# A fused transformer block on one core: the attention's second product moves to the end of a slot of the layers, and its output projection behind the next tile's projection of q

## What is computed

```python
for i in range(6):
    t = shift_tokens(x)                       # half the channels come from the token before
    q, k, v = split(t @ Wqkv[i])              # 128 -> 3 * 1024
    q, k = rotary(l2norm(q) * qs), rotary(l2norm(k) * ks)
    x = local_attention(q, k, v) @ Wo[i] + x  # softmax over 64 keys, 1024 -> 128
    n = layernorm(shift_tokens(x)) * g + b
    a, gate = split(n @ W1[i] + b1)           # 128 -> 2 * 341
    x = (a * gelu(gate)) @ W2[i] + b2 + x
x = x_mid + gb * x
```

## Time and profile before

| | us |
|---|---|
| median of 3 runs | 3675.78 |
| lowest and highest | 3674.07 to 3676.65 |
| profiled execution, its own time | 3676.79 |
| span of its profile | 3675.0 |
| busy in the span: PE | 3518.1 (96%) |
| DVE | 3185.6 (87%) |
| ACT | 2870.5 (78%) |
| POOL | 2576.6 (70%) |

### The profile page before, as it was taken

The page is one execution under the profiler, slowest core; times in us unless marked ns, Lnnn a source line. Parts: engine busy times, 40 slices in busy tenths (PEclk is TensorE's granted clock), DMA queues, the critical chain, the costliest instruction groups (busy, mean ns, idle before and its releaser), DMA issues.

```text
span 3675.0 us, 161687 instructions
## 1 busy us (share of the span) xinstructions
PE 3518.1 (96%) x70540; PEld 2666.8 (73%) x70540; DVE 3185.6 (87%) x4422; ACT 2870.5 (78%) x5288; POOL 2576.6 (70%) x2106
## 2 busy tenths in 40 slices
PE   6999999869999999999999999999999999999996
PEld 2222222358888888888888888888888888888885
DVE  7999999578888988888888889888888888888884
ACT  3999999857777787877777787878777777777774
POOL 3222111278888888888888888888888888888883
PEclk8999999989999999999999999999999999999999
DMA  4110000034444444444444444444444444444432
GB/s 121 40 42 22 23 20 19 16 96 111 122 115 110 126 116 117 117 113 114 128 115 120 113 115 127 113 118 114 114 122 120 117 118 111 132 119 111 115 111 73
DMA packets 210250, 366.48 MB, mean 100 GB/s; under 512 B 37106, under 2 KB 81734, under 8 KB 209222
## 3 DMA queue, kind: packets, MB, share of 16 engines
q1 hardware_dynamic: 209482, 355.05, 35.1%
HBM read 236.73 MB, written 111.67 MB: 95 GB/s over the span
## 4 chain that ended last, share of the span: by engine, by line
PE 46%; DVE 14%; ACT 9%; issue 5%; POOL 5%; ACTq 0%; POOLq 0%; DVEq 0%
PE PB L1447 8%; PE PA L1371 8%; PE PD L1399 6%; PE PD L1460 5%; PE PB L1371 4%; PE PC L1421 4%; PE PC L1499 3%; DVE T L1756 3%; PE PA L1430 3%; PE PC L1475 2%; POOL T L1283 2%; DVE T L1746 2%; DVE T L1750 2%; DVE ss L1762 2%; ACT Vs L1565 1%
## 5 line engine op out<-in xcount | busy, mean ns | idle before, releaser
L1265 POOL TENSOR_TENSOR T<-T 128x1024 f32<-128x1024 f32 x384 | 907.3, 2379 | 8.7 <-DVE T L1756 8.7
L1283 POOL TENSOR_TENSOR T<-T,rn 128x1024 f32<-128x1024 f32 x384 | 731.4, 1905 | 27.7 <-POOL rn L1276 1.3
L1371 PE MATMUL PA<-Wqkv,XS 128*128 128x512 f32 x2304 | 633.0, 410 | 9.8 <-DVE XS L1710 9.1
L759 DVE TENSOR_REDUCE negmax<-p_max 128x1 f32<-128x1024 f32 x512 | 588.9, 1214 | 15.5 <-PE p_max L659 13.4
L821 ACT ACTIVATE E<-p_low 128x512 f32<-128x512 f32 x1024 | 554.0, 596 | 27.7 <-PE p_low L683 16.9
L1371 PEld LDWEIGHTS PA<-Wqkv,XS 128*128 128x128 f32 x2304 | 417.0, 194 | 80.7 <-DVE XS L1710 10.7
L1728 DVE TENSOR_REDUCE sm<-Ew 128x16 f32<-128x1024 f32 x192 | 233.6, 1217 | 236.7 <-ACT Ew L1589 236.7
L1762 DVE TENSOR_REDUCE ss<-SQ 128x32 f32<-128x2048 f32 x192 | 436.9, 2276 | 0.0
L1399 PE MATMUL PD<-ident,T 128*128 128x128 f32 x3072 | 410.7, 277 | 17.5 <-POOL T L1283 16.2
L1447 PEld LDWEIGHTS PB<-ET,VW 64*64 64x64 f32 x24576 | 376.4, 135 | 45.6 <-DVE T L1756 29.6
L1447 PE MATMUL PB<-ET,VW 64*64 64x32 f32 x24576 | 398.2, 220 | 10.6 <-DVE T L1756 5.2
(11 more groups left out here) (167 smaller groups left out, 6988.7 us busy)
## 6 DMA issues: line engine op xcount, KB each, us to landing
VW<-v_rows SPq DMA_DIRECT2D x768, 256.0 KB, 4.6
v_rows<-Vs SPq DMA_DIRECT2D x192, 512.0 KB, 3.4
Wraw<-in_Wqkv SPq DMA_DIRECT2D x40, 192.0 KB, 5.0
QA<-parts_q SPq DMA_DIRECT2D x384, 16.0 KB
KA<-parts_k SPq DMA_DIRECT2D x192, 32.0 KB
fs<-XC SPq DMA_DIRECT2D x48, 127.0 KB
parts_q<-AO SPq DMA_DIRECT2D x8, 384.0 KB, 2.6
parts_k<-AO SPq DMA_DIRECT2D x8, 384.0 KB, 3.3
```

The costliest lines, as they stand in the source:

```text
L759: dve.tensor_reduce(negmax[:, qh, c, qt:qt + 1], p_max[:, k % 2, :], axis=AX.X, op=ALU.max, negate=True).then_inc(s_mr.sem, 1)
L1265: pool.tensor_tensor(out=t_, in0=t_, in1=T2[:, i * HALF:(i + 1) * HALF], op=ALU.add).then_inc(ad.sem, 1)
L1283: pool.tensor_tensor(out=t_, in0=t_, in1=rn[:, p, i * LH:(i + 1) * LH].unsqueeze(2).broadcast_to([P, LH, LD]), op=ALU.mult).then_inc(no.se ...
L1371: mm = pe.matmul(pair[:, half, :], XS[:, b, i, 1:P + 1], Wqkv[:, l % 2, j, lo:lo + 512], start=(k == 0), stop=(k == 2))
```

## The change

On PE `attend(s-3)` goes from behind the transposition of k to the slot's end, behind `project_v` and the feed-forward's products of the slot. `output(s-4)` goes from ahead of `project_qk(s, 0)` to behind it, and the alignment goes with it. On ACT `project_v` and `exponentials` now come ahead of `attend`, and `roots` behind it. On DVE `output` stands behind the first half of `rotate`. SP waits for the output of tile `s-4` rather than for scores ahead of its transfers, and for the first copy of qT rather than the third copy (kT) ahead of reading the windows. No computation is added or removed.

```diff
@@ on_sp
-            if is_tile(s - 2):
-                sp.wait_ge(sc.sem, sc.at(s - 2))
+            if is_tile(s - 4):
+                sp.wait_ge(wo.sem, wo.at(s - 4))
             if is_tile(s - 1):
                 values_out(s - 1)
-                sp.wait_ge(te.sem, te.at(s - 1, 3))
+                sp.wait_ge(te.sem, te.at(s - 1, 1))
@@ layers
-    BLOCK, FIRST_Q = 256, (105, 105, 98, 98)
+    BLOCK, FIRST_OUT = 256, (51, 41, 39, 19)
@@ on_pe, project_qk
             if i == 0:
-                pe.addr_align(BLOCK, offset=FIRST_Q[b], max_nops=0)
                 pe.wait_ge(xl.sem, xl.at(n))
@@ on_pe, output
             u, b, t, l = tile(n)
+            pe.addr_align(BLOCK, offset=FIRST_OUT[b], max_nops=0)
             free(fd[0])
@@ on_pe, the loop
+            if is_tile(s):
+                project_qk(s, 0)
             if is_tile(s - 4):
                 output(s - 4)
-            if is_tile(s):
-                project_qk(s, 0)
...
                 transpose_qk(s - 1, 1)
-            if is_tile(s - 3):
-                attend(s - 3)
             if is_tile(s + 1):
                 input_T(s + 1)
...
                 ff_down(u - 2)
+            if is_tile(s - 3):
+                attend(s - 3)
@@ on_act, the loop
+            if is_tile(s):
+                project_v(s)
+            if is_tile(s - 2):
+                exponentials(s - 2)
             if is_tile(s - 3):
                 attend(s - 3)
             if is_tile(s):
-                project_v(s)
                 roots(s)
             if d == 0 and is_step(u - 2):
                 ff_norm(u - 2)
-            if is_tile(s - 2):
-                exponentials(s - 2)
@@ on_dve, the loop
+            if is_tile(s):
+                rotate(s, 0)
             if is_tile(s - 4):
                 output(s - 4)
...
             if is_tile(s):
-                rotate(s, 0)
                 rotate(s, 1)
```

More of the change, by code:

```diff
@@ L1696, in on_act @@
                 ff_norm(u - 2)
-            if is_tile(s - 2):
-                exponentials(s - 2)
-            if d == 0 and is_step(u - 2):
                 ff_high(u - 2)
```

## The result

| | before | after |
|---|---|---|
| median, us | 3675.59 | 4087.86 |
| lowest and highest | 3674.07 to 3676.65 | 4083.45 to 4095.98 |
| span of the profile | 3675.0 | 4094.2 |

The changed kernel takes 1.1125 times as long, interval [1.1105, 1.1144], that is 412 us more. The forecast was 301 more. The direction and the largest term were right, the sum was 111 us short, and the time lies above the range.

What follows compares the result with a forecast made beforehand. PE was taken to set the pace, busy 2469.7 of 2500 us in the layers. Terms 265 + 31 + 10 + 10 - 15 = 301 us on 3676.8 gave 3978, median forecast 3977 us; range for 8 in 10: 3880 to 4055 us.

Steps and rivals of the forecast that it cites:

- The wait for kH: On PE, `input_T` waits for ACT's kH copy out of PD once `attend` moves: 1.40 us, 189 slots, 265 us.
- Scores with d = 3: PE's scores wait for DVE's last `ff_value` product, now behind the rotation of q: 0.64 us in 48 steps, 31 us.
- The branch and SP's transfers: PE's one branch a slot stays at 0.29 us and SP's earlier window reads cost nothing: 0 us.
- whether OT is ready: `output` behind the projection of q: ACT's OT copy is covered by some 0.4 us, so no cost by itself.
- Roots behind the copy: ACT's roots wait for `attend`'s copy, delaying POOL's `normalise` and PE's transposition of k at d = 3: +10 us net.
- gates: At d = 2 ACT's gates queue behind OT; cost to PE taken as 0.2 us a step, +10 us.
- what comes back: PE's wait for POOL's divided exponentials and some other idle time should go: -15 us, between 0 and -50.
- POOL's loop: Rival: the closed loop of roots, POOL, transposition of k, kH, `input_T`, `project_v`, `attend`, OT sets the pace; 4063 us, chance 0.12.
- Wait alone: Rival: `input_T` waits, but POOL and DVE gain time, no other wait appears, holes close; 3882 us, chance 0.15.
- The clock falls: Rival: PE idles once every slot, so a quarter of each slot runs at half speed; 4545 us, chance 0.04.
- the piece from 771 to 792 us: Evidence against a falling clock: PE busy only 13.3 of 21 us, two waits of 1.39 us, yet clock 1.00.

Runs made afterwards that it cites:

- the first experiment: Kernel before with one edit: on PE `input_T` goes ahead of `attend`, which stays ahead of `project_v`; 4054.03 us, 1.1025.
- the reduction: Changed kernel with DVE's copy of X's upper half written as a maximum over an axis of length 1; 4046.62 us, 1.1002.
- the earlier release: Changed kernel with kH copied from kT instead of PD, so PD is free one copy sooner; 4090.43 us, 1.1124.
- the last experiment: Changed kernel with two edits: `input_T` behind `project_v`, and DVE's copy of X as a maximum over a length-1 axis; 3881.05 us, 1.055.

## Why the prediction was partly right

**The wait for kH: right.** Forecast 1.40 us for 189 slots, 265 us; the list shows 263.9 us in 190 waits, and the steps between groups give 265. Slots 1 and 2 of the kernel before had shown the number. The first experiment gave it again in another order.

**Scores with d = 3: the mechanism was right, the term too small.** Forecast 31 us, measured 72. The sum took DVE's output and the copy of X as 0.52 us from the earlier trace rows, where the copy starts just ahead of POOL's division. In its new place behind the rotation it starts 0.8 us into that division, ends after it, and takes 1244 instead of 309 ns. That is 0.93 us a step, 44 us, and the reduction gave 41 back.

**The branch and SP's transfers: the step "nothing for either" failed for the branch.** The count of instructions is indeed the same, but 0.29 us was the branch's cost at its old place, not a price of a branch. At its new place its median is 1.88 us, and PE does not get `output`'s instructions in time: 51 us. Moving it by 40 instructions restores the step's length. For SP's transfers nothing was right as far as the runs go: no wait for VW is in the list, and leaving out most of their bytes changed nothing clear of noise; no run restores SP's old order. The prediction had asked of `output` only whether OT is ready; that part held (OT is not among the larger waits after).

**POOL and ACT: too high, and small.** Roots behind the copy (10), gates (10) and what comes back (-15) were forecast as +5. The waits for POOL's T went from 16.2 to 13.9 us and the steps of the transpositions are 6 us shorter. POOL's loop did not become the pace.

**Not foreseen at all: 29 us** in groups of the feed-forward, k, v and output that each got a little longer. I have no run that isolates them.

With these, 265 + 72 + 51 + 29 - 6 = 411 stands against 301 = 265 + 31 + 0 + 5. That the largest term came out to the microsecond does not make the sum right: the misses are the scores' wait (41 short), the late instructions (51 short) and the rest (29 short, 11 too many). The list says where the time stood and not what each removal is worth: taking out the 265 gave 116, taking out the 51 gave 9 to 26.

**The rivals.** "Wait alone" fell, since 3882 would need every other wait to vanish. "The clock falls" did not happen on any scale in the changed kernel (twelve falls of some 3 us in the layers, mean 1.00), as the piece from 771 to 792 us had suggested. But the chance rested on one arrangement: the clock fell 39 times behind the same wait of 1.39 us in the first experiment, and 30 times behind a wait of 2.0 us in the one with the earlier release. The price in that rival, 4545 us, was far too high: 74 us in the first case, and in the second, with the longer wait of the scores, the time that the shorter wait at `input_T` had saved. The Trainium skill's case in "TensorE: Matmul & The Clock Gate", section "A second HAM failure mode: psum-queue depth-cycling", has a kernel whose clock goes down and up as short idle pieces come between its groups of matmuls; these two runs agree with that, and the changed kernel mostly does not.

**What stays open.** Half of the 412 us was removed by two edits; that the rest is late instructions and the small waits of the last experiment is read from its list, not shown by a run. The new orders on ACT and SP were not run alone. What decides whether a wait is followed by a fall of the clock is open too: it is not the length alone, since the 37 waits of the scores of up to 2.3 us with `input_T` behind `project_v` led to 10 falls, and 37 of 2.0 us to 30. Why the instructions come late at one place of the block and not at another is only argued: `attend` and the scores issue 128 matmuls and 128 weight loads each in some 2 us, a whole block of 256, and the large waits for instructions that were found stand in one of them or in one of the next groups.

## What to carry to other kernels

Before work is moved away from a PSUM bank's hand-over, look for what covers the copies out of that bank: the idle time that appears could be read here from the timeline beforehand (1.39 us a slot). Price each neighbour at its new place, not at its old: a DVE copy that starts under a GpSimd product waits for its end, while one that starts just ahead of it does not, and the same branch cost 0.29 or 1.88 us by its place. After a wait is removed, look at what was hidden behind it before counting the gain: here 265 us of wait were worth 116.

## What the runs showed of the hardware

**Two engines at SBUF.** A DVE copy of 128x256 elements took 0.29 us where it started 0.02 us ahead of a product of POOL, which then took 2.03 instead of 1.90 us. Started while the product ran it took 1244 to 1839 ns in the mean of a run, ending 0.15 us after it. In the changed kernel's place an operation with two SBUF inputs took 1383 ns, a reduction 420 ns.

**Instructions that come late.** PE waited for instructions for up to 2.2 us at a time even inside groups and without a branch: 147 us in 2500 with the offsets at 164, 65 without a branch. The page of the profile after lists the queue that fetches them (packets, MB, share of the engines):

```profile
q8 instruction: 627, 10.27, 1.1%
```

That is 16.4 KB a packet. The Trainium skill, "Runtime: NRT & Kernel Launch", section "Instruction fetch mechanics", has fetches of 16 KiB blocks of 256 instructions, with which this agrees, and calls the cost of crossing a block mostly hidden. There the measurement decides: in and behind groups that issue 256 instructions in about 2 us it was not hidden here.

**The clock.** TensorE stayed at 2.4 GHz, but for twelve falls, through 190 waits of 1.39 us with a projection behind each, and went to 1.2 GHz in 39 slots where `attend` followed the same wait. Behind waits of the scores of 2.0 us it fell 30 times in 37, behind ones of 0.76 never.
